# Second attention: the softmax division done by a masked copy, a partition shuffle and a wide reciprocal instead of two 32x32 transposes

## The reference

```python
q = q * jax.nn.sigmoid(unity_scale)
scores = jnp.einsum('bhqd,bhkd->bhqk', q, k) / jnp.sqrt(jnp.asarray(D, x.dtype))
allowed = (j % STRIDE == 0) | (jnp.abs(i - j) <= LOCAL)      # STRIDE 4, LOCAL 8
scores = jnp.where(allowed, scores, -jnp.inf)
attn = jax.nn.softmax(scores, axis=-1)
out = jnp.einsum('bhqk,bhkd->bhqd', attn, v)
out = out.transpose(0, 2, 1, 3).reshape(B, S, H)
return out @ o_w + o_b
```

## Time and profile before

| | |
|---|---|
| median of 3 runs | 1629.59 us (1628.52 to 1632.96) |
| profiled execution | 1629.59 us, of which the span of the trace is 1628.4 us |
| PE busy | 1527.2 us (94%) |
| PEld busy | 1113.8 us (68%) |
| DVE busy | 981.0 us (60%) |
| ACT busy | 986.6 us (61%) |
| POOL busy | 830.2 us (51%) |
| granted TensorE clock, mean | 0.984 of full speed |

### The profile page before, as it was taken

One profiled execution on the slowest core, in us unless ns is written; L12 is line 12 of the kernel. 1 busy time (PEld: TensorE's weight loads), 2 busy tenths in 40 slices (PEclk: granted clock), 3 DMA queues, 4 the chain that ended last, 5 costly groups with the idle time before them and its releaser, 6 DMA issues.

```text
span 1628.4 us, 46789 instructions
## 1 busy us (share of the span) xinstructions
PE 1527.2 (94%) x18055; PEld 1113.8 (68%) x18059; DVE 981.0 (60%) x2063; ACT 986.6 (61%) x2039; POOL 830.2 (51%) x908
## 2 busy tenths in 40 slices
PE   7999999999999999999999979899998999999895
PEld 5555445555555889889777756666666999997663
DVE  6788898787775212121499967856655222224887
ACT  5767676767766445444454556677776545546773
POOL 7334488888874545454212200177774555553433
PEclk9999999999999999999999979999999999999998
DMA  9910002000103889888334310011112544432434
GB/s 312 417 62 1 9 30 100 28 29 31 31 28 77 218 219 243 231 215 233 117 102 138 88 56 2 8 50 47 47 47 47 98 89 90 100 80 81 132 106 124
DMA packets 296955, 169.45 MB, mean 104 GB/s; under 512 B 198081, under 2 KB 273217, under 8 KB 293793
## 3 DMA queue, kind: packets, MB, share of 16 engines
q1 hardware_dynamic: 277312, 128.45, 30.2%
q0 software_dynamic: 16832, 34.64, 6.2%
q10 hardware_dynamic: 2592, 3.38, 0.7%
HBM read 96.74 MB, written 69.63 MB: 102 GB/s over the span
## 4 chain that ended last, share of the span: by engine, by line
PE 59%; POOL 12%; issue 10%; DVE 8%; ACT 4%; DMA 4%; SPq 3%; POOLq 0%; DVEq 0%; ACTq 0%
PE ps L1862 13%; PE ps L1871 13%; POOL xd L623 6%; POOL s_S L656 4%; PE ps L1675 4%; PE ps L1766 4%; DVE s_RS L1341 4%; PE ps L1903 4%; PE ps L1803 4%; PE ps L1891 3%; ACT s_PX L882 3%; DMA s_W<-in_ew 2%; PE ps L1699 2%; SPq L460 2%; PE ps L1813 2%
## 5 line engine op out<-in xcount | busy, mean ns | idle before, releaser
L623 POOL DMA_INDIRECT xd<-s_XN,s_slots x256 | 251.3, 982 | 84.0 <-issue 62.4
L816 ACT ACTIVATE s_S<-ps 128x512 f32<-128x512 f32 x384 | 208.4, 595 | 141.5 <-PE ps L1675 141.5
L1529 DVE TENSOR_TENSOR s_PP<-ps,s_S 128x1024 f32<-128x1024 f32 x192 | 234.5, 1221 | 74.2 <-PE ps L1675 52.6
L1675 PE MATMUL ps<-s_QM,s_KK 32*128 32x512 f32 x1536 | 233.9, 639 | 2.7 <-ACT s_S L816 2.7
L897 ACT ACTIVATE s_HH<-ps,s_LG 128x256 f32<-128x256 f32 x284 | 125.8, 473 | 136.6 <-PE ps L1862 136.6
L640 POOL DMA_INDIRECT yd<-s_Y,s_to x142 | 135.9, 957 | 137.9 <-DVE s_Y L1471 113.5
L882 ACT ACTIVATE s_PX<-ps,s_scl 128x1024 f32<-128x1024 f32 x128 | 135.5, 1110 | 110.9 <-PE ps L1813 110.9
L656 POOL TENSOR_SCALAR_AFFINE_SELECT s_S<-s_S 128x1024 f32<-128x1024 f32 x128 | 140.5, 1098 | 114.5 <-ACT s_S L816 113.8
L1341 DVE TENSOR_REDUCE s_RS<-ps 128x8 f32<-128x1024 f32 x128 | 150.3, 1216 | 63.0 <-PE ps L1770 63.0
L897 ACT ACTIVATE s_XN<-ps,s_b1s 128x256 f32<-128x256 f32 x256 | 113.3, 473 | 115.2 <-PE ps L1862 111.2
L640 POOL DMA_INDIRECT yd<-s_XN,s_to x128 | 122.5, 957 | 117.8 <-DVE s_XN L1471 95.8
(11 more groups left out here) (220 smaller groups left out, 2709.8 us busy)
## 6 DMA issues: line engine op xcount, KB each, us to landing
s_W<-in_ew SPq DMA_DIRECT2D x71, 576.0 KB
s_X<-xd SPq DMA_DIRECT2D x540, 32.0 KB
xd<-s_zero SPq DMA_DIRECT2D x16, 1056.0 KB, 18.1
s_YG<-yd SPq DMA_DIRECT2D x32, 256.0 KB, 3.7
s_XN<-yd SPq DMA_DIRECT2D x32, 256.0 KB, 3.7
yd<-s_zero SPq DMA_DIRECT2D x7, 1056.0 KB, 27.9
s_XN<-in_x SPq DMA_DIRECT2D x8, 512.0 KB, 7.3
xd<-s_XN,s_slots POOLq DMA_INDIRECT x256
```

Of the source, the lines that this page charges most:

```text
L623: e.indirect_dma_start(out=xd, out_offset=bass.IndirectOffsetOnAxis(ap=m.slots[:, k, i:i + 1], axis=0), in_=m.XNp[:, i, 0:C + 1], in_offse ...
L816: e.mul(m.S1[u % 3][:, t * 512:(t + 1) * 512], m.PA[:, t * 512:(t + 1) * 512], 1.0 / 64.0).then_inc(s.ev1, 1)
L1529: e.tensor_tensor(m.PP[u % 4][:], m.PB[u % 2], m.S1[u % 3][:], ALU.mult).then_inc(s.prod, 1)
L1675: return e.matmul(out, m.KK[k][32 * r:32 * r + 32, kind, kc * P:(kc + 1) * P], m.QM[k][32 * r:32 * r + 32, kind, :, qc * P:(qc + 1) * P], ...
```

## The change

ScalarE gets a new instruction per block, `second_halves`, that copies bank 6 to SBUF (SEC) and multiplies it by a column that is 1 on partitions 16 to 31 of each 32 and 0 elsewhere. DVE then puts together the denominators (DEN: on the lower 16 partitions from the second half of bank 6, on the upper 16 from SEC) and in the same way the numerators (NUM), swaps the two groups of 16 partitions of DEN with one stream shuffle, takes the reciprocal of all 128x256 values, and multiplies. The two transposes are gone; the reciprocal is of 256 values per partition instead of 32. The final DVE instruction is the same step in the program as before (it signals `yn`).

```diff
--- before.py
+++ after.py
@@ -217,6 +217,7 @@
     m.tix = small[:, 72:144]
     m.pcol = small[:, 144:145]
     m.eoff = small[:, 146:154]
+    m.first_half, m.second_half = small[:, 158:159], small[:, 159:160]
     m.row = small[:, 160:302]
     m.mk = [small[:, 154 + j:155 + j] for j in range(4)]
     lg_words = m.LG[:].rearrange("p i e -> p (i e)")
@@ -328,7 +329,7 @@
     m.KS.append(sbx(bt, "KS2", [P, 576]))
     m.K4.append(sbx(bt, "K41", [P, 4, 320]))
     m.Q4.append(sbx(bt, "Q41", [P, 4, 256]))
-    m.YM = sbx(bt, "YM", [P, 256])
+    m.RC = sbx(bt, "RC", [P, 256])
     m.YC = sbx(bt, "YC", [P, 256])
     r.O = sbx(bt, "r1O", [P, 2, NT, E], BF16)
     r.O2 = r.O[:].rearrange("p k i e -> p (k i) e")
@@ -347,8 +348,8 @@
     x.W = [sbx(bt, f"W1_{k}", [P, 2, 512]) for k in range(2)]
     x.X = [sbx(bt, f"X1_{k}", [P, 2 * ROW]) for k in range(6)]
     m.b1s, m.b2s = sbx(bt, "b1s", [P, E, 4]), sbx(bt, "b2s", [P, E, C])
-    m.TM = sbx(bt, "TM", [P, 512])
-    m.RC = sbx(bt, "RC", [P, 32])
+    m.SEC = sbx(bt, "SEC", [P, 512])
+    m.DEN, m.NUM = sbx(bt, "DEN", [P, 256]), sbx(bt, "NUM", [P, 256])
     bt.close()
 
     xn_words = m.XNp[:].rearrange("p i c -> p (i c)")
@@ -422,7 +423,7 @@
         "zw", "zv", "xw", "qp", "kp", "vp", "qs", "ks", "vn", "q4", "k4"))
     s.scl_a, s.scl, s.max, s.maxv, s.neg, s.mturn, s.mvt = (sem(n) for n in (
         "scl_a", "scl", "max", "maxv", "neg", "mturn", "mvt"))
-    s.sc, s.ex, s.wv, s.yn, s.o1, s.given = (sem(n) for n in ("sc", "ex", "wv", "yn", "o1", "given"))
+    s.sc, s.ex, s.wv, s.sec, s.yn, s.o1, s.given = (sem(n) for n in ("sc", "ex", "wv", "sec", "yn", "o1", "given"))
     s.zg = [sem(f"l_zg{k}") for k in range(NF)]
     s.zx = [sem(f"l_zx{k}") for k in range(NF)]
     s.out = [sem(f"l_out{k}") for k in range(NF)]
@@ -881,6 +882,14 @@
             e.wait_ge(s.wv, n - 1)
         e.activation(m.PX[hp][:, 2 * half:2 * half + 2, :].rearrange("p r n -> p (r n)"),
                      m.ps[:, (2 + 2 * half) * 512:(4 + 2 * half) * 512], ACT.Exp, scale=m.scl[:, 0:1]).then_inc(s.ex, 1)
+
+
+def second_halves(e, m, s, b):
+
+    e.wait_ge(s.wv, 2 * b + 2)
+    if b >= 1:
+        e.wait_ge(s.yn, b)
+    e.mul(m.SEC[:], m.PS[6][:, 0:512], m.second_half).then_inc(s.sec, 1)
 
 
 def expert_act(e, m, s, x, n, func, bias):
@@ -1020,6 +1029,8 @@
             e.activation(m.LG[:], m.LG[:], ACT.Exp).then_inc(s.gate_exp, 1)
         if t < 2:
             end_act(e, m, s, NG - 2 + t, 1)
+        if 1 <= t < NB and t - 1 != MOE_AFTER:
+            second_halves(e, m, s, t - 1)
         if t < NB:
             exponents(e, m, s, t, 0)
         if t < 2:
@@ -1042,7 +1053,10 @@
             queries_copy(e, m, s, t + 3)
         for p in pairs_combined(t)[1]:
             tanh_last(e, m, s, p)
+        if t == NB:
+            second_halves(e, m, s, NB - 1)
         if t == MOE_AFTER:
+            second_halves(e, m, s, t)
             expert_act(e, m, s, m.x1, 1, ACT.Relu, lambda i, j: m.b1s[:, i // 8, j:j + 1])
 
 
@@ -1360,19 +1374,18 @@
 
 def divide_second(e, m, s, o, b):
 
-    e.wait_ge(s.wv, 2 * b + 2)
-    o.mark(e.transpose(m.TM[:], m.PS[6]))
-    o.wait()
-    o.mark(e.reciprocal(m.RC[:].rearrange("p (b h x) -> p b h x", b=8, h=2), view(m.TM[:], 16, [[32, 8], [240, 2], [8, 2]])))
-    o.wait()
-    for hp in range(2):
-        value = view(m.TM[:], 272 * hp, [[32, 8], [8, 2], [1, 8]])
-        one_over = view(m.RC[:], 2 * hp, [[4, 8], [1, 2], [0, 8]])
-        o.mark(e.tensor_tensor(view(m.YM[:], 16 * hp, [[32, 8], [8, 2], [1, 8]]), value, one_over, ALU.mult))
+    first, second = m.PS[6][:, 0:256], m.PS[6][:, 256:512]
+    e.wait_ge(s.sec, b + 1)
+    den = o.mark(e.scalar_tensor_tensor(m.DEN[:], second, m.first_half, m.SEC[:, 0:256], ALU.mult, ALU.add))
+    o.mark(e.scalar_tensor_tensor(m.NUM[:], first, m.first_half, m.SEC[:, 256:512], ALU.mult, ALU.add))
+    o.wait(den)
+    o.mark(e.stream_shuffle(m.RC[:], m.DEN[:], [i ^ 16 for i in range(32)]))
+    o.wait()
+    o.mark(e.reciprocal(m.RC[:], m.RC[:]))
     o.wait()
     if b >= 1:
         e.wait_ge(s.o1, b)
-    e.transpose(m.YC[:], m.YM[:]).then_inc(s.yn, 1)
+    e.tensor_tensor(m.YC[:], m.NUM[:], m.RC[:], ALU.mult).then_inc(s.yn, 1)
 
 
 def keep_second(e, m, s, b):
@@ -2105,6 +2118,8 @@
     sm[:, 160:302] = np.arange(P)[:, None] + P * np.arange(142)[None, :]
     for j in range(4):
         sm[:, 154 + j] = (np.arange(P) // 8) % 4 == j
+    sm[:, 158] = (np.arange(P) // 16) % 2 == 0
+    sm[:, 159] = (np.arange(P) // 16) % 2 == 1
     c["c_small"] = sm
     c["c_tok"] = np.tile(NX1 * SL + np.arange(2 * NT, dtype=f) * P, (P, 1)).astype(f)
     inv = (f(1.0) / np.power(f(10000.0), np.arange(0, 8, 2, dtype=f) / f(8))).astype(f)
```

## The result

| | before | changed |
|---|---|---|
| median of six runs each, us | 1631.14 | 1641.11 |
| lowest to highest, us | 1628.52 to 1633.38 | 1637.23 to 1644.84 |
| profiled execution, us (span) | 1629.59 (1628.4) | 1639.27 (1638.0) |

The ratio is 1.0067 [1.0052, 1.0083]: slower by about 10 to 11 us, against a forecast of 1643.1 us.

The account below looks back on a forecast made before the run. The chain was taken as mostly TensorE's, 59% of the span, with 8% on DVE. Terms 1.5 + 5.5 + 2.8 + 0 + 3.2 + 0.5 = 13.5 us on 1629.59 gave 1643.1 us, range 1637 to 1651.

Parts of the forecast that it names:

- third rival: Wide reciprocal runs two columns in the time of one, division only 0.58 us longer: 1633.9 us; chance 0.05.
- (a): Steps 1 to 21 and block 21: 1.37 us more against 1.36 us room, a tie; 1.5 us charged.
- first rival: DVE sequence longer than summed, tie lost in each early block: 1651 us; chance 0.18, shared with the ACT-copy rival.
- (b): Steps 24, 27, 29, 30: final-sum work precedes `keep_second`, so all 1.37 us passes on; 5.5 us.
- (c): Steps 23, 26, 28: `keep_second` waits about 0.4 us, which hides that much of the delay; 2.8 us.
- (d): Step 25 costs nothing: a 1.05 us stretch vanishes and a 0.69 us DMA wait absorbs the rest.
- (e): Step 31 and the end: ACT copy on the path, YC 1.85 us later, last division adds 1.37; together 3.2 us.
- (f): Final-sum portions in (b) move to where POOL copies its windows: 0.5 us, between -2 and +2 us.
- second rival: The final sum takes the delay up as DVE stalls against POOL fall away: perhaps 5 us back, 1638 us; chance 0.12.

Follow-up runs that it names:

- the longer division: The changed kernel with one more DVE reciprocal of 32 columns, into a spare tile, in the division: 1649.65 us, ratio 1.0119; on a slower chip 1698.71 us, ratio 1.0093.

## Why the prediction was right

**The division.** Forecast 3.48 us, measured 3.47 to 3.48, each part within its own bounds: the two scalar_tensor_tensor 0.475 and 0.473 us (0.48), the shuffle 0.436 (0.45), the reciprocal 1.753 (1.75), the product 0.427 (0.42). The groups by shape, to be put beside the earlier trace rows:

```profile
L1384 DVE RECIPROCAL s_RC<-s_RC 128x256 f32<-128x256 f32 x32 | 56.1, 1753 | 1.1
L1379 DVE SCALAR_TENSOR_TENSOR s_DEN<-ps,s_small,s_SEC 128x256 f32<-128x256 f32 x32 | 15.2, 475 | 4.2 <-ACT s_SEC L892 4.2
L1380 DVE SCALAR_TENSOR_TENSOR s_NUM<-ps,s_small,s_SEC 128x256 f32<-128x256 f32 x32 | 15.1, 473 | 0.0
L1382 DVE STREAM_SHUFFLE s_RC<-s_DEN 128x256 f32<-128x256 f32 x32 | 13.9, 436 | 0.0
L1396 DVE TENSOR_TENSOR s_RS<-ps,s_RS 128x256 f32<-128x256 f32 x31 | 13.1, 422 | 20.4 <-PE ps L1854 20.4
```

The repeat count of 8 in the Trainium skill, "VectorE: DVE Perf Modes", "First, the fixed hardware budget", would by the prediction's estimate have made 2.13 us of the reciprocal; the run has 1.75. The third rival (two columns in the time of one, under 1.05 us) is out by the same row.

**(a) Early blocks.** Forecast 1.5 us for 21 blocks, measured +1.1 for 19. The tie held but in step 6, the one that the prediction named as having less room: `keep_second` waited 53.9 us in all before and 20.4 after, so 33.5 of the 32 x 1.37 = 44 us that DVE works longer went into idle time of this one instruction. The first rival needed 0.3 us more in the sequence. It did not come. The lane selection that spoke for it (the Trainium skill, "Vector Engine (DVE) Microarchitecture Reference", "The reshape front-end and per-opcode configuration") is there as an instruction of its own, and the timeline above gives it 0.01 us. But the longer division shows that its mechanism was real and its price right: 0.19 us per block for 0.21.

**(b), (c), (d) Late blocks.** By step, forecast and measured in us:

| step | 23 | 24 | 25 | 26 | 27 | 28 | 29 | 30 | sum |
|---|---|---|---|---|---|---|---|---|---|
| forecast | 0.9 | 1.4 | 0 | 0.9 | 1.4 | 0.9 | 1.4 | 1.4 | 8.3 |
| measured | 0.78 | 1.87 | -0.83 | 0.77 | 1.53 | 0.71 | 1.40 | 2.12 | 8.35 |

In step 27 the whole of the longer division passed on to the reductions (2.78 us from YC to `keep_second`, as before), and the runs with `keep_second` first show that these are what TensorE waits for. (b) came to 6.9 instead of 5.5 and (c) to 2.3 instead of 2.8. For step 25 I had the pair's stretch of 1.05 us vanish, and it did. Another of 1.02 us appeared in step 24, in a portion of the final sum. DVE and POOL after:

```profile
1519.61 2.15 DVE L1410 SCALAR_TENSOR_TENSOR s_XN<-s_XN,s_wgt 128x128 f32<-128x128 f32 x4
...
1525.82 1.75 DVE L1384 RECIPROCAL s_RC<-s_RC 128x256 f32<-128x256 f32 x1
1527.61 0.42 DVE L1388 TENSOR_TENSOR s_YC<-s_NUM,s_RC 128x256 f32<-128x256 f32 x1
```

```profile
1520.25 1.36 POOL L1429 TENSOR_TENSOR s_XN<-s_XN,s_RS 128x512 f32<-128x512 f32 x1 [3.75 <-PE ps L1728]
1521.69 1.80 POOL L1432 TENSOR_TENSOR s_XN<-s_XN 128x512 f32<-128x512 f32 x1
```

Four instructions that take 1.13 us elsewhere take 2.15 here, beside POOL's sum. That the two belong together is read from times that overlap; no run separates them. Steps 24 and 25 together are +1.04 us against the 1.4 forecast. The stretch of step 24 belongs to this execution: with the new division late on the slower chips step 24 took 14.51 or 14.52 us and had none, +1.35 on 13.17.

That the sums agree to 0.1 us is partly luck. The eight intervals took 106.5 and 107.4 us with the old division on chips of 1631 us and 115.8 with the new one, and 108.3 against 117.8 on chips of 1682 us with slow scores in step 25 on both sides: the late cost is 8.4 to 9.5 us by the pair of executions taken.

**(e) The end.** Step 30 has 0.7 us more than forecast and step 31 as much less: the ledger counts the wait for the new copy on ScalarE to step 30.

```profile
DVE s_RS L1355 <- PE ps L1783: 6.2, 5, 2.5
DVE s_DEN L1379 <- ACT s_SEC L892: 3.5, 1, 3.5
```

These are DVE's largest waits after 1500 us (total, times, longest). The wait of 2.74 us has become 3.46, +0.72 for the copy of 0.69 us, where the prediction had 0.66 with the handovers for a copy of 0.6. Steps 30, 31 and the end together: forecast 1.4 + 1.85 + 1.37 = 4.6, measured 2.12 + 1.19 + 1.29 = 4.6. TensorE idled 9.69 us for the last YC instead of 8.62, and the last product starts 6.43 us behind the end of the last portion instead of 5.07, 1.36 us later as forecast.

**The copy's cover.** The prediction had the copy done 0.4 us before DVE wants it. It started up to 0.38 us behind the end of `weigh` and took 0.69 us, so in some blocks 0.03 us were left. Nothing was lost by it, but the cover was nearly used up, which the prediction did not see.

**(f) POOL.** Charged with +0.5 us, range -2 to +2. Stretches did move, and no run separates what that cost or gave. The second rival, which wanted 5 us back, would have left the late steps 3.3 us longer; they are 8.4.

**The size.** Forecast 13.5 us; 11.9 in the two profiled executions without the three pieces that vary between executions, 11 by the ratio. Against the forecast, (a) is 0.4 lower, (b) 1.4 higher, (c) 0.5 lower, (d) 0.8 lower, (e) 0.7 lower and (f), of which nothing can be seen beside (b) and (d), 0.5 lower. The largest of them, in (b), (d) and (e), are in part shifts between neighbours: a stretch gone in step 25 and one more in step 24, the wait for the copy counted to step 30 instead of 31. The mechanisms of (a), (b), (c) and (e) were right. (d) rests on a stall that moves between executions: step 25 took 15.59 and 14.55 us with the old division and 14.76 with the new one, and with slow scores 16.83 against 16.45 and 16.74, so that it cost next to nothing, as forecast, but by the two terms named only in part: on the slower chips DVE still waited 0.24 and 0.38 us for the DMA. (f) can't be seen. That errors of up to 1.4 us leave 1.6 us in the sum is in part that they offset each other.

## What to carry to other kernels

Price a longer step by its room in each stage: here the same 1.37 us costs 0.03 us where another engine is late by as much, 0.58 in the one step where that engine is less late, 0.7 to 0.8 where its own engine has 0.4 us of idle time behind it, and 1.4 to 1.5 where it has none. A tie is worth a run of its own with a little more on top, since it tells whether the next edit is free. And before work is moved out of the way of a waiting instruction, look at what the next engine really waits for: here it was the instruction after it.

## What the runs showed of the hardware

- A reciprocal costs 353, 554, 932 and 1753 ns for 32, 64, 128 and 256 columns: 6.3, 5.9 and 6.4 ns for each further column. The other passes of this division take 1.7 to 1.9 ns a column, all told.
- The lane selection ahead of the shuffle (LOAD_MASK_SELECT) takes 6 to 15 ns, and the shuffle of 128x256 takes 436 ns, less than the transpose of that shape (0.45 us).
- ScalarE's copy out of PSUM with a factor per partition takes 687 ns for 128x512, against the 595 ns of the earlier trace rows. A nearer row stood in the trace of the kernel before: L907, also 128x512 out of PSUM with one operand value per partition, 687 ns.
- After 2.95 us of idle time inside one block (`keep_second` first, step 27) TensorE's granted clock was 0.50 from 1610 to 1612 us, the level of 1.2 GHz, and 0.55 on average over 3.8 us; before it was 1.00 (2.4 GHz). 32 products took 2.09 instead of 1.17 us. The length of the idle time alone does not tell: after 2.09 us in step 25 of the kernel before the clock stayed at 1.00, after 2.02 us in the same step with the new division early only it fell.
- The chips differ by 3% (1631 and 1682 us), and 44 of the 51 us lie between the divisions of blocks 1 and 20 (296.2 us with the new division early, 252.5 for the same kernel on the other kind). On the slow ones steps 7 to 20 take 15.2 to 19.4 us, and TensorE halts inside the 64 products of `weigh` with nothing named that it waits for. The timeline of the kernel with the new division late only:

```profile
1140.12 1.04 PE L1871 MATMUL ps<-s_PX,s_VN 128*32 128x64 f32 x31
1141.61 0.69 PE L1871 MATMUL ps<-s_PX,s_VN 128*32 128x64 f32 x33 [0.44 <-issue]
```

These are the steps in which POOL issues the scatter of rows for the experts. What makes a chip behave so stays open; the ratios of the changed kernel on both kinds (1.0067 and 1.0083) agree within their intervals.
